# Two-layer cross-attention on one core: layer-1 softmax row sums from ScalarE's accumulator output in place of VectorE reductions

## The reference, cut to what matters

```python
scores = jnp.einsum('bhqd,bhkd->bhqk', Q, K) / np.sqrt(D_K)   # D_K = 32, 77 keys
attn = jax.nn.softmax(scores, axis=-1)
context = jnp.einsum('bhqk,bhkd->bhqd', attn, V)
output = context.transpose(0, 2, 1, 3).reshape(B, Sq, D_MODEL) @ W_o.T + b_o
x = output + query        # then layer norm
```

## Time and profile before

| | us |
|---|---|
| median of 3 executions | 414.82 |
| lowest, highest | 413.18, 416.59 |
| profiled execution, its own time | 413.24 |
| its span from first to last instruction | 411.4 |
| TensorE busy | 390.6 |
| VectorE busy | 289.6 |
| ScalarE busy | 261.4 |
| GpSimd busy | 218.3 |

### The profile page before, as it was taken

The page is one execution under the profiler, slowest core; times in us unless marked ns, Lnnn a source line. Parts: engine busy times, 40 slices in busy tenths (PEclk is TensorE's granted clock), DMA queues, the critical chain, the costliest instruction groups (busy, mean ns, idle before and its releaser), DMA issues.

```text
span 411.4 us, 12169 instructions
## 1 busy us (share of the span) xinstructions
PE 390.6 (95%) x4968; PEld 295.9 (72%) x4968; DVE 289.6 (70%) x707; ACT 261.4 (64%) x779; POOL 218.3 (53%) x242
## 2 busy tenths in 40 slices
PE   3999999699999999999999999999999999999994
PEld 3896855478777877777768777777777776777663
DVE  0135577558866888669866996688867986657787
ACT  0423777676658675895588665867589558776820
POOL 0310258423547754776537754775477654773541
PEclk9999999999999999999999999999999999999999
DMA  7994104400015210423042401520052301252022
GB/s 249 399 336 143 59 2 134 140 11 2 3 38 190 84 48 2 175 80 104 0 148 82 130 2 40 188 104 28 2 175 83 101 2 31 78 154 79 2 102 102
DMA packets 19229, 39.44 MB, mean 96 GB/s; under 512 B 1865, under 2 KB 5449, under 8 KB 18151
## 3 DMA queue, kind: packets, MB, share of 16 engines
q1 hardware_dynamic: 18599, 37.72, 26.7%
q10 hardware_dynamic: 576, 0.96, 0.7%
HBM read 26.49 MB, written 8.39 MB: 85 GB/s over the span
## 4 chain that ended last, share of the span: by engine, by line
PE 83%; DMA 6%; ACT 5%; DVE 3%; SPq 2%; issue 1%; DVEq 0%
PE ps_q L907 21%; PE ps_out L972 19%; PE ps_t L932 13%; PE ps_s L921 7%; PE ps_pv L947 7%; PE ps_out L868 4%; DMA p_b<-p_l 4%; PE ps_s L844 4%; SPq L274 2%; PE ps_s L990 2%; ACT prob L488 1%; ACT pt L497 1%; PE ps_pv L881 1%; DMA raw<-in_w0k 1%; PE ps_pv L844 1%
## 5 line engine op out<-in xcount | busy, mean ns | idle before, releaser
L350 POOL TENSOR_TENSOR prob<-prob,rc 128x308 f32<-128x308 f32 x128 | 91.2, 719 | 142.1 <-DVE rc L677 141.9
L488 ACT ACTIVATE prob<-ps_s,mx 128x77 f32<-128x77 f32 x512 | 121.7, 323 | 0.7 <-DVE mx L668 0.7
L497 ACT ACTIVATE pt<-ps_t 77x512 f32<-77x512 f32 x128 | 76.2, 596 | 62.2 <-PE ps_t L932 61.5
L675 DVE TENSOR_REDUCE sm<-prob 128x4 f32<-128x308 f32 x128 | 59.5, 465 | 36.5 <-ACT prob L488 36.5
L932 PE MATMUL ps_t<-ident,prob 128*77 128x128 f32 x512 | 79.2, 277 | 2.3 <-ACT pt L497 2.3
L932 PEld LDWEIGHTS ps_t<-ident,prob 128*77 128x77 f32 x512 | 61.7, 147 | 20.4 <-issue 6.3
L668 DVE TENSOR_REDUCE mx<-ps_s 128x4 f32<-128x308 f32 x128 | 54.6, 469 | 25.0 <-PE ps_s L921 24.9
L329 POOL TENSOR_TENSOR x_l<-x_raw,x_h 128x512 fp32r<-128x512 f32 x32 | 44.3, 1389 | 25.5 <-ACT x_h L441 15.3
L907 PE MATMUL ps_q<-x_h,wq_h 128*128 128x512 f32 x128 | 53.5, 418 | 0.0
L907 PE MATMUL ps_q<-x_h,wq_l 128*128 128x512 f32 x128 | 53.1, 415 | 0.0
L921 PEld LDWEIGHTS ps_s<-k1T,q 32*64 32x64 f32 x2048 | 25.8, 130 | 27.5 <-issue 14.7
(11 more groups left out here) (114 smaller groups left out, 592.7 us busy)
## 6 DMA issues: line engine op xcount, KB each, us to landing
x_raw<-in_xT SPq DMA_DIRECT2D x8, 1024.0 KB, 6.1
y<-in_x SPq DMA_DIRECT2D x28, 256.0 KB, 2.7
out<-y SPq DMA_DIRECT2D x28, 256.0 KB, 2.0
p_b<-p_a SPq DMA_DIRECT2D x8, 154.0 KB
mask_sb<-in_mask SPq DMA_DIRECT2D x7, 154.0 KB, 5.5
raw<-in_w0k SPq DMA_DIRECT2D x2, 512.0 KB, 6.8
raw<-in_w0q SPq DMA_DIRECT2D x2, 512.0 KB, 10.3
raw<-in_w0v SPq DMA_DIRECT2D x1, 1024.0 KB, 12.5
```

What stands on the lines that cost most here:

```text
L350: nc.gpsimd.tensor_tensor(ap, ap, wide(rc[:, k % 2, h], KEYS), ALU.mult).then_inc(prob_done, 1)
L488: e = nc.scalar.activation(prob[:, k % 2, h, t], ps_s[:, h, t * KEYS:(t + 1) * KEYS], ACT.Exp, bias=mx[:, k % 2, h, t:t + 1])
L497: nc.scalar.activation(pt[:, h], ps_t[0:KEYS, :], ACT.Copy).then_inc(pt_ready, 1)
L675: nc.vector.reduce_sum(sm[:, k % 2, h], prob[:, k % 2, h], AX_X).then_inc(sum_done, 1)
```

## The change

`exps` gives each of its ACTIVATEs an accumulator output, `accum_out`, which writes the row sums of the 77 exponentials of one head and tile into `sm`. `inverse_sums` loses its reduction and the wait for that reduction. The reciprocal now follows the wait for `exp_done` directly.

```diff
                 for t in range(TILES):
-                    e = nc.scalar.activation(prob[:, k % 2, h, t], ps_s[:, h, t * KEYS:(t + 1) * KEYS], ACT.Exp, bias=mx[:, k % 2, h, t:t + 1])
+                    e = nc.scalar.activation(prob[:, k % 2, h, t], ps_s[:, h, t * KEYS:(t + 1) * KEYS], ACT.Exp,
+                                             bias=mx[:, k % 2, h, t:t + 1], accum_out=sm[:, k % 2, h, t:t + 1])
                 e.then_inc(exp_done, 1)
```

```diff
                 wait(dve, exp_done, heads(i, k, h) + 1)
-                nc.vector.reduce_sum(sm[:, k % 2, h], prob[:, k % 2, h], AX_X).then_inc(sum_done, 1)
-                wait(dve, sum_done, heads(i, k, h) + 1)
                 nc.vector.reciprocal(rc[:, k % 2, h], sm[:, k % 2, h]).then_inc(rcp_done, 1)
```

## The result

The changed kernel takes 423.63 us (median of 4 executions, 422.19 to 423.99) against 414.81 us before: ratio 1.0205, 95% interval 1.0157 to 1.0253. The profiled execution took 423.99 us with a span of 422.2; before it was 413.24 and 411.4. So the profile to explain is 10.8 us longer, the medians 8.8. The forecast was 427, with 12.0 us between the profiled executions. One execution of the first run with both sums (638.86 us) and one of the kernel before beside it (769.48 us) fell into a slow state and count in no ratio and in no median here.

What follows compares the result with a forecast made beforehand. TensorE was taken as the bound, busy 95%. A block grows by 28r - 0.8 = 1.7 us, seven blocks by 12.0; on 413.24 that gives 425.3, and with 1.6 for the median 427 us, range 415 to 463.

Steps and rivals of the forecast that it cites:

- The bound and the place: TensorE bounds at 95% busy; in g = 3 and g = 0 ScalarE is at most 0.3 us behind being the bound.
- VectorE's sums are worth nothing: Removing 59.5 us of sums from VectorE gives back 0, at most 1.7 us from two single waits.
- r = 0.09: Start-to-start time that delivering a sum adds to each ScalarE exponential: 0.09 us, with ends 0.05 and 0.27.
- Rival A: The extra accumulator read on ScalarE drains the pipeline: 0.12 to 0.2 us each, centre 0.17, 446 us; chance 0.25.
- B: Nothing overlaps on ScalarE, which becomes the bound in all four steps: about 0.27 us each, 477 us; chance 0.10.
- C: The sum leaves with the ACTIVATE: under 0.03 us each, not slower, 415 us or 413; chance 0.10.
- 16r - 0.6: Growth of a step g = 0: 16 exponentials up to the end of `round_q`, less 0.6 us of slack.
- 12r - 0.2: Growth of a step g = 3: 12 exponentials behind the second `pt` copy, less 0.2 us of slack.
- The first block and the end, counted as nothing: The first block's steps have no `normalise` and the end has no `round_q`, so both were taken to add nothing.
- The sum: Growth of the tight steps g = 0 and g = 3 over seven blocks: 12.0 us on the profiled execution.
- g = 1 and g = 2 do not pay at 0.09: Growth 8r - 1.4 in g = 1, nothing below 0.18; 8r - 0.8 in g = 2, nothing below 0.10.
- ScalarE's idle time before `pt` falls by some 30 us: Sign of a right forecast: ScalarE's idle time before the `pt` copies, 61.5 us, falls by some 30.

Runs made afterwards that it cites:

- both sums: Changed kernel with VectorE's sums put back into a tile nobody reads, run twice: 424.92 us (1.0244) and 424.66 us (1.0245).
- g = 0 and 3: Kernel before with row sums by ScalarE's accumulator in steps g = 0 and g = 3, by VectorE in the others: 422.69 us, ratio 1.0205.
- g = 3 only: Kernel before with row sums by ScalarE's accumulator in steps g = 3, by VectorE in the others: 420.65 us, ratio 1.0154.
- g = 1 and 2: Kernel before with row sums by ScalarE's accumulator in steps g = 1 and g = 2, by VectorE in the others: 415.45 us, ratio 1.0024.
- `round_q` moved: `round_q` put ahead of the one `normalise` before it in g = 3 and g = 0: kernel before 415.23 us (1.0016), changed kernel 418.81 us (1.0103).
- the small copy: Kernel before with a 128x1 ScalarE copy in front of each exponential, in place of the accumulator output: 424.26 us, ratio 1.0239.
- no sums at all: Kernel before with VectorE's sums removed and nothing in their place, reciprocals taken of the row maxima: 414.51 us, ratio 1.0002.
- g = 0 only: Kernel before with row sums by ScalarE's accumulator in steps g = 0, by VectorE in the others: 417.38 us, ratio 1.0059.
- reads and small copies: Changed kernel with a further 128x1 ScalarE copy in front of each exponential, 512 in all: 458.90 us, ratio 1.1057.

## Why the prediction was right, point by point

- **The bound and the place.** Right. TensorE is the bound, ScalarE has slack by its share but next to none in the steps g = 3 and g = 0, and from the second block on only these grow. The runs with 256 reads in either pair of steps show it: 1.0024 against 1.0205. But one part of the evidence was luck. The prediction read the weight loader's 14 waits on `round_q` as two steps in each of seven blocks. By the timeline of before they stand in front of the scores of k = 2 and k = 4 and, in pairs, of k = 8 and 9, 12 and 13, and so on to 28 and 29: six pairs and two single ones. Most of these waits are 0.84 us long, and so are most of those that end by `issue`, for example in front of k = 2 and k = 6:

```profile
62.78 0.80 PEld L921 LDWEIGHTS ps_s<-k1T,q 32*64 32x64 f32 x64 [0.84 <-ACT q L459]
...
103.81 0.79 PEld L921 LDWEIGHTS ps_s<-k1T,q 32*64 32x64 f32 x64 [0.84 <-issue]
```

  So their number is not a measure of the slack; the distance from the copy's end to the scores is, which the prediction took from the timeline. It is 0.31 us at the end of the steps g = 0 from k = 8 to 24, but 1.01 at the end of k = 4, which has no `normalise` in front of the copy, and 0.05 at that of k = 28. At the end of the steps g = 3 it is 0.05 or 0.20, three times each.
- **VectorE's sums are worth nothing.** Right, by the run without them (1.0002) and the run with both (within 1.0 us of the changed kernel).
- **r = 0.09.** Right: 0.30 - 0.21 us from the trace. I had bracketed it between ScalarE's 0.05, got by subtracting columns, and VectorE's 0.10 for a small instruction. ScalarE's own small copy has 0.09, so the subtraction was low. Rival A (0.17) and B (0.27), a pipeline that drains, fall by the read's start-to-start distance; C (the sum leaves for free) falls by the 512 rows. The estimate worked out in the prediction from the Trainium skill, ScalarE: Activation LUTs, section What ACT_TABLE_LOAD costs, was 0.094 us; the trace agrees with its 0.09. The Trainium skill, VectorE: DVE Perf Modes, section Two Vector instructions with no wait between them, says that a VectorE op that writes out its accumulator is two instructions; the 512 reads show the same here on ScalarE.
- **16r - 0.6 and 12r - 0.2.** The terms were too large: 0.84 and 0.88 were forecast for a step, 0.57 and 0.67 to 0.81 measured. This is the term that the prediction mis-sized: the slack. I took the idle times of the earlier trace rows at their face, 0.15 and 0.16 us. But an idle time counts from the end of the row before, and ScalarE starts the next instruction 0.11 us ahead of that end when it need not wait. Start to start, each pause is worth 0.26, and the fourth head, which shows no idle time at all, still had 0.92 - 0.84 = 0.08 (0.84 being four exponentials at 0.21). That makes the slack 0.26 + 0.27 + 0.08 + 0.31 = 0.92 in g = 0 and 0.15 + 0.11 + 0.06 = 0.32 in g = 3, and the growth 16 x 0.09 - 0.92 = 0.52 and 12 x 0.09 - 0.32 = 0.76, close to what was measured. In g = 3 the row read was one of the three with 0.05 us behind the copy; these grew by 0.80 to 0.81, the three with 0.20 by 0.67 to 0.68. The two steps g = 0 at the ends, k = 4 and k = 28, were not like the one read either, and grew by 0.19 and 0.34.
- **The first block and the end, counted as nothing.** Wrong by 1.0 us in the first block, where k = 0 and k = 2 pay. The formula has seven steps g = 3, though without the first block and the end only six are left (k = 7 to 27). The seventh is k = 31, which grew 1.1 where 0.88 was forecast, but by another path, since no `round_q` stands there: TensorE waits for `pt` copies (the wait in front of the `context` in that step went from 0.24 to 0.61 us) and then 0.28 us for GpSimd's second scaled head.
- **The sum.** Forecast 7 x (0.84 + 0.88) = 12.0 us; measured 4.4 (of which 1.0 is the pause at k = 16) for g = 0, 4.5 + 1.1 for g = 3, 1.0 for the first block, -0.2 ahead of it. The slack was read too small by 0.4 us a block, some 3 us, and the first block and the pause, 2 us, make up for a good part of it. Without them the forecast would have been further off, so its closeness is in part luck. The median forecast of 427 is 3.2 us too high: 1.2 from this sum, and 2.0 because I added the 1.6 us by which the profiled execution of before lay below its median, while that of the changed kernel lay 0.4 above.
- **g = 1 and g = 2 do not pay at 0.09.** Right from the second block on, 0.0 us over 14 steps; in the first block k = 2 does.
- **ScalarE's idle time before `pt` falls by some 30 us.** It fell by 15, from 61.5 to 46.4, and 103 pauses became 49. Another 8 us went from the wait in front of the context's copy `ct_h` (37.7 to 29.8). ScalarE's idle time in the whole span fell by 27 us, from 411.4 - 261.4 = 150.0 to 422.2 - 298.8 = 123.4.

Open stays why the step k = 16 is about 1 us longer than the other steps g = 0 of the same kernel in some profiles (the changed kernel both times, both sums, g = 0 and 3, g = 3 only, g = 1 and 2, and the variants of the kernel before with `round_q` moved and with the small copy) and not in others (the kernel before, no sums at all, g = 0 only, the changed kernel with `round_q` moved). Two of those that have it are no slower than the kernel before by their medians, so it is not the reads as such. One thing goes with it. In the profiles that have it, the first 16 KB transfer inside the step on the queue q8, whose kind is `instruction`, starts 6.5 to 6.9 us behind the step's start; in the four that do not have it, 3.2 to 3.3 us behind. The DMA view of the changed kernel from 5.5 to 8.1 us into the step, and of the kernel before from 2.5 to 4.5:

```profile
q8 instruction: 1, 0.02, 2.8%
```

```profile
q8 instruction: 1, 0.02, 2.7%
```

In the run with reads and small copies that transfer starts at 7.5 us, and TensorE pauses in the same matmuls too, by 0.77 us, though the step is no longer for it. Whether the late transfer is the cause is not shown: no run was made for it.

No version beat the kernel before. The nearest that computes the same is the kernel before with `round_q` moved (1.0016), then the one with reads only in g = 1 and g = 2 (1.0024); both are the same as the kernel before within the measurement.

## What to carry to other kernels

Moving work off an engine that is busy 70% can gain nothing while adding 0.09 us at a time to one that is busy 64% costs 2%: look at which engine is late in front of the bound engine's waits, step by step, and count what stands in front of that one instruction. Read from the timeline which steps the waits belong to; a count that happens to match is no proof. An accumulator output on many short ScalarE instructions cost a whole small instruction each here, 0.09 us beside the 0.21 of an exponential of 77 columns. On longer rows its share should be smaller; no run here tried that. When slack is read from idle times, add the overlap that the engine would have had (0.11 us on ScalarE here), since an idle time starts at the end of a row and not where the next instruction could have started.

## What the runs showed of the hardware

The read of ScalarE's accumulator is an instruction of its own with a row of 217 ns, which delays the next ACTIVATE by 0.09 us; a 128x1 copy on ScalarE has 213 ns and 0.09 us. Not expected was the clock in the run with reads and small copies: after steps g = 3 in which TensorE was busy almost alike (11.45 us of 13.20, and 11.49 of 13.21), both at full clock, the step g = 0 behind was granted 0.86 once and 1.00 the other time. These are the rows of the two steps g = 3; those of the steps g = 0 behind them are shown with that run:

```profile
175.03:188.23 13.20, 11.45 (x125) 7.89 (x121) 5.99 (x15) 11.58 (x58) 6.04 (x8) 1.00 0.34 117
...
225.54:238.75 13.21, 11.49 (x125) 7.89 (x121) 5.98 (x15) 11.58 (x58) 6.03 (x8) 1.00 0.33 116
```

What decides between them was not found.
